# A fused stack of graph layers: another order of blocks on every engine, another table of PSUM banks, another order of loads

## What is computed

```
h  = relu(LN(x));   H = (adj != 0)
x1 = x + hypergraph_conv(LN(relu(hypergraph_conv(h; W1))); W2) + h     # "L0": D^-1 H B^-1 H^T (x W^T)
x2 = x1 + elu(softmax_masked(leaky(a1.Wh + a2.Wh)) Wh),  h = relu(LN(x1))          # "L1", mask adj > 0.5
x3 = x2 + relu(h W0 + T h W1 + T T h W2 + b), T = adj*exp(leaky(si+sj)) normalised  # "L2", h = relu(LN(x2))
x4 = x3 + w v,  w = softmax over nodes of sum_m(q k^T / 8 * adj), h = relu(LN(x3))   # "L3"
```

## Time and profile before

| | |
|---|---|
| median of 3 runs | 1487.95 us (1487.61 to 1488.96) |
| the profiled execution, span | 1487.0 us |
| mean granted TensorE clock | 0.989 |
| busy: PE, DVE, ACT, POOL | 96%, 81%, 66%, 64% |

### The profile page before, as it was taken

The page is one execution under the profiler, slowest core; times in us unless marked ns, Lnnn a source line. Parts: engine busy times, 40 slices in busy tenths (PEclk is TensorE's granted clock), DMA queues, the critical chain, the costliest instruction groups (busy, mean ns, idle before and its releaser), DMA issues.

```text
span 1487.0 us, 33717 instructions
## 1 busy us (share of the span) xinstructions
PE 1423.5 (96%) x8920; PEld 1263.7 (85%) x8920; DVE 1206.8 (81%) x4621; ACT 978.8 (66%) x2122; POOL 949.7 (64%) x974
## 2 busy tenths in 40 slices
PE   6799999999999999999999999999999999999975
PEld 5679988889888988988888988888988888988864
DVE  5778888888888888888888888888888888888773
ACT  4456667766667776667776666776666776666754
POOL 4555775666776666676666676675677666677524
PEclk9899999999999999999999999999999999999997
DMA  4001111101111110111110111110111110111001
GB/s 128 22 15 37 37 42 44 49 32 46 35 48 36 49 47 30 35 49 35 49 49 28 42 42 35 49 49 28 45 39 35 49 49 28 49 35 41 23 29 50
DMA packets 75372, 62.01 MB, mean 42 GB/s; under 512 B 3014, under 2 KB 70986, under 8 KB 75339
## 3 DMA queue, kind: packets, MB, share of 16 engines
q1 hardware_dynamic: 75338, 61.63, 12.7%
HBM read 36.45 MB, written 16.78 MB: 36 GB/s over the span
## 4 chain that ended last, share of the span: by engine, by line
PE 75%; ACT 11%; issue 5%; DVE 5%; DMA 1%; POOL 0%; DVEq 0%; ACTq 0%; POOLq 0%; SPq 0%
PE ps L343 35%; PE ps L347 18%; PE ps L328 16%; PE ps L491 4%; ACT wh L851 3%; ACT pT L940 3%; ACT h L918 2%; ACT h2T_hi L881 1%; ACT p L929 1%; PE ps L400 1%; ACT yT_hi L953 1%; DMA x_in<-in_x 1%; DVE stats L1329 1%; DVE h L1347 1%; DVE binc_T L1368 0%
## 5 line engine op out<-in xcount | busy, mean ns | idle before, releaser
L1130 POOL TENSOR_TENSOR x3n<-p,x 128x512 f32<-128x512 f32 x64 | 80.8, 1285 | 252.8 <-ACT p L929 252.8
L851 ACT ACTIVATE p<-ps,rs 128x512 f32<-128x512 f32 (+1 forms) x256 | 138.2, 582 | 106.4 <-PE ps L347 73.7
L1090 POOL TENSOR_TENSOR hT_lo<-hT,hT_hi 128x512 fp32r<-128x512 f32 x126 | 162.8, 1294 | 68.5 <-ACT hT_hi L871 65.4
L1085 POOL TENSOR_TENSOR rs<-var_e,neg_half 128x4 f32<-128x4 f32 x160 | 164.9, 1031 | 23.7
L343 PE MATMUL ps<-wl_hi,h2T_hi 128*128 128x258 f32 (+1 forms) x512 | 148.5, 371 | 7.8 <-ACT h2T_hi L881 7.2
L328 PE MATMUL ps<-p,alT 128*128 128x256 f32 (+1 forms) x512 | 136.9, 390 | 3.3 <-DVE h3T_lo L1239 2.3
L343 PE MATMUL ps<-wl_lo,h2T_hi 128*128 128x258 f32 (+1 forms) x512 | 132.9, 341 | 0.0
L347 PE MATMUL ps<-wl_hi,h2T_lo 128*128 128x258 f32 (+1 forms) x512 | 132.4, 340 | 0.0
L949 ACT ACTIVATE h3T_hi<-ps 128x512 fp32r<-128x512 f32 x64 | 38.0, 594 | 139.0 <-PE ps L491 138.9
L491 PE MATMUL ps<-ident,h 128*128 128x128 f32 x768 | 118.3, 278 | 9.9 <-DVE h L1347 9.4
L491 PEld LDWEIGHTS ps<-ident,h 128*128 128x128 f32 x768 | 92.3, 142 | 32.9 <-issue 10.4
(11 more groups left out here) (178 smaller groups left out, 4476.0 us busy)
## 6 DMA issues: line engine op xcount, KB each, us to landing
x_in<-in_x SPq DMA_DIRECT2D x32, 512.0 KB, 3.9
out_x<-x SPq DMA_DIRECT2D x32, 512.0 KB, 2.9
adj_f<-in_adjT SPq DMA_DIRECT2D x32, 256.0 KB, 2.9
adj_m<-in_adjT SPq DMA_DIRECT2D x32, 256.0 KB, 2.8
adj_l<-adj_m SPq DMA_DIRECT2D x32, 256.0 KB, 2.3
vqk<-in_l_wk SPq DMA_DIRECT2D x3, 256.0 KB, 5.2
x<-in_w2T SPq DMA_DIRECT2D x1, 512.0 KB, 5.1
x<-in_w1T SPq DMA_DIRECT2D x1, 512.0 KB, 5.9
```

The costliest lines, as they stand in the source:

```text
L851: return act.activation(dst, src, ACT.Copy, scale=scale)
L1085: pool.tensor_tensor(rs[:, layer, :], var_e[:, layer, :], neg_half[:], ALU.pow).then_inc(done, G)
L1090: pool.tensor_tensor(hTs[1][:, hc, :], hT[:, hc, :], hTs[0][:, hc, :], ALU.subtract).then_inc(S["hT_lo"], 1)
L1130: pool.tensor_tensor(x3n[:, s], p0[:, s], x2[:, s], ALU.add).then_inc(S["x3_ready"], 2)
```

## The change

No arithmetic is added or taken away on any engine, apart from how it is cut (relu of p0 in two halves on ACT; each layer norm in two halves of two groups; one more memset for each half).

- PE: the blocks of a round stand in another order (below). Round 0 has its own list, `opening`, in the old order with `first_rows` behind `front_w1(0)`.
- DVE: `elu`, layer norm 2, `mid_low`, layer norm 3, the pooling sums, `mid_columns`, `late_low(0)` and `tail_norm` are done for the coming round at the end of the body (`ahead`); `front_penalty` becomes `next_penalty` and is done one round earlier; count, inverse, binc and moments come first in the body.
- ACT: `copy_h2T(0)` moves ahead of `copy_u(2)`, the copies of vqk 2 and 3 behind the softmax, `copy_p2(3)` behind the exponentials of the edges, `keep_wh(3)` ahead of `copy_yT`, half of relu of p0 ahead of `keep_wh(1)`, the other half behind vqk 3.
- POOL: `add_res0` and `add_x3` of the round before come first; the power pair of the next group stands behind that of the hidden layer and ahead of `mask_edges`; `add_bias` ahead of `add_x4`, both `add_xb` last.
- BANK: every product has other banks, and the waits of PE's blocks follow from the table: for example `mid_p10(2)` waits for `zb_ready`, `late_vqk(0)` for `deg_ready`, `late_vqk(2)` for `wh_kept` 3, `next_y(0)` for `wh_kept` 1, `mid_p2(3)` for `p10_copied` 1 (as before), `front_w1(3)` for the copy of u 0, `front_w1(0)` for both low halves of y.
- SP: the loads wait for the penalty alone in the steady rounds; the order becomes `adj_f`, adj_m to adj_l, `x_in`, store, `adj_m`.

```diff
     PAIRS = G // 2
-    FIRST_STEADY = 4
+    FIRST_STEADY = 6
+    LAST_SHIFT = 4
     ATT = wqkT.shape[1] // 2
     assert C == P and G * C == 512 and GROUPS > FIRST_STEADY + 1
...
         """.split()
         S = {n: sem(n) for n in names}
 
-        BANK = {"u": (0, 4, 3, 2), "y": (0, 7), "s": (4, 5), "d": (0,), "c2": (6, 5), "h1": (7, 1), "wh": (2, 3, 4,
-    5), "b1": (6,), "att": (1, 5), "h2": (4, 3), "p2": (4, 5, 6, 7), "p10": (7, 6, 7, 6), "b2": (5,),
-    "z": (1, 2, 3, 4), "ap": (0, 1, 2, 3), "az": (0, 3), "h3": (0, 5), "vqk": (4, 1, 6, 7), "ak": (6,),
-    "row": (1,), "turn": (7,)}
+        BANK = {"u": (3, 6, 0, 3), "y": (0, 3), "s": (5, 6), "d": (7,), "c2": (0, 7), "h1": (1, 5),
+    "wh": (0, 1, 2, 3), "b1": (5,), "att": (1, 2), "h2": (5, 6), "p2": (2, 3, 4, 5),
+    "p10": (5, 7, 6, 0), "b2": (6,), "z": (0, 1, 2, 3), "ap": (1, 2, 3, 4), "az": (6, 4),
+    "h3": (7, 4), "vqk": (5, 7, 2, 6), "ak": (7,), "row": (6,), "turn": (5,)}
 
         def bank(name, k=0):
...
+        wait(sp, S["al_ready"], r.mid(G))
+    if not r.steady and r.i in (GROUPS - 2, GROUPS - 1, GROUPS,):
+        wait(sp, S["ak_ready"], r.late(G))
+    sp.dma_start(adj_l[:], adj_m[:]).then_inc(S["adj_l_loaded"], 16)
+
+def load_mask(r):
+    if r.steady or r.i > 0:
+        sp.wait_ge(S["adj_l_loaded"], r.loads(r.i - 1))
+    sp.dma_start(adj_m[:], group(adjT, r.i)).then_inc(S["adj_m_loaded"], 16)
+
 def body(r):
-    if r.has_next:
-        if r.steady or r.i >= 0:
-
-            wait(sp, S["pen_ready"], r.front(G))
-            wait(sp, S["binc_ready"], r.front(G))
-            sp.dma_start(adj_f[:], group(adjT, r.i + 1)).then_inc(S["adj_f_loaded"], 16)
-            wait(sp, S["h0_ready"], r.front(G))
-            wait(sp, S["xb_ready"], r.front(G))
-            sp.dma_start(x_in[:], group(x, r.i + 1)).then_inc(S["x_loaded"], 16)
-    if r.has_tail:
-        wait(sp, S["x4_ready"], r.tail(G))
-        sp.dma_start(group(out, r.i - 3), x4[:]).then_inc(S["stored"], 16)
-    if r.has_mid:
-
-        wait(sp, S["al_ready"], r.mid(G))
-        wait(sp, S["ak_ready"], r.late(G))
-        sp.dma_start(adj_l[:], adj_m[:]).then_inc(S["adj_l_loaded"], 16)
-        sp.wait_ge(S["adj_l_loaded"], r.loads(r.i - 1))
-    if r.has_front:
-        sp.dma_start(adj_m[:], group(adjT, r.i)).then_inc(S["adj_m_loaded"], 16)
-
-rounds(sp, body)
+    past = r.later(-1)
+    if r.has_next:
+        load_adj(r)
+    if past.has_mid:
+        hand_adj(past)
+    if r.has_next:
+        load_x(r)
+    if past.has_tail:
+        store(past)
+    if past.has_front:
+        load_mask(past)
+
+def opening(r):
+    load_adj(r)
+    load_x(r)
+
+rounds(sp, body, opening)
 sp.wait_ge(S["stored"], 16 * GROUPS)
 
...
@@ -734,79 +619,77 @@
         front_w1(r, 0)
         front_w1(r, 1)
         front_w1(r, 2)
+    if r.has_mid:
+        mid_h2(r, 0)
+    if r.has_front:
         front_w1(r, 3)
     if r.has_mid:
-        mid_h2(r, 0)
         mid_h2(r, 1)
+        mid_p2(r, 0)
         mid_p10(r, 0)
+        mid_p2(r, 1)
+    if r.has_front:
+        front_w2(r, 0)
+    if r.has_mid:
+        mid_p2(r, 2)
+    if r.has_late:
+        late_h3(r, 0)
     if r.has_tail:
         tail_row(r)
     if r.has_mid:
-        mid_p2(r, 0)
-        mid_p2(r, 1)
-        mid_p2(r, 2)
         mid_p2(r, 3)
     if r.has_front:
-        front_w2(r, 2)
-    if not r.steady and r.i == 0:
-        second_rows(r)
-        first_weights(r)
-    if r.has_front:
-        front_w2(r, 0)
+        front_w2(r, 1)
     if r.has_mid:
         mid_b2(r)
     if r.has_front:
-        front_w2(r, 3)
-        front_w2(r, 1)
         front_w2_low(r, 0)
         front_w2_low(r, 1)
+        front_w2(r, 2)
+        front_w2(r, 3)
         front_w2_low(r, 2)
+        front_w2_low(r, 3)
         front_sums(r, 0)
         front_sums(r, 1)
         front_sums(r, 2)
-        front_w2_low(r, 3)
         front_sums(r, 3)
-    if r.has_mid:
-        mid_p10(r, 1)
-    if r.has_late:
-        late_h3(r, 0)
-    if r.has_mid:
-        mid_p10(r, 2)
     if r.has_late:
         late_h3(r, 1)
     if r.has_mid:
-        mid_ap(r, 0)
-        mid_ap(r, 1)
+        mid_p10(r, 1)
     if r.has_tail:
         tail_turn(r)
     if r.has_mid:
+        mid_p10(r, 2)
+    if r.has_front:
+        front_c2(r, 0)
+        front_c2(r, 1)
+        front_c2(r, 2)
+    if r.has_next:
+        next_s(r, 0)
+        next_s(r, 1)
+    if r.has_mid:
+        mid_ap(r, 0)
+    if r.has_front:
+        front_c2(r, 3)
+    if r.has_mid:
+        mid_ap(r, 1)
         mid_ap(r, 2)
         mid_ap(r, 3)
-    if r.has_front:
-        front_c2(r, 0)
-        front_c2(r, 1)
+        mid_p10(r, 3)
     if r.has_late:
         late_vqk(r, 0)
     if r.has_front:
-        front_c2(r, 2)
-        front_c2(r, 3)
-    if r.has_mid:
-        mid_p10(r, 3)
+        front_h1(r, 0)
     if r.has_late:
         late_vqk(r, 1)
-    if r.has_next:
-        next_s(r, 0)
     if r.has_mid:
         mid_az(r, 0)
+    if r.has_front:
+        front_h1(r, 1)
+    if r.has_mid:
         mid_az(r, 1)
-    if r.has_next:
-        next_s(r, 1)
-    if r.has_front:
-        front_h1(r, 0)
-    if r.has_late:
-        late_vqk(r, 2)
-    if r.has_front:
-        front_h1(r, 1)
+    if r.has_front:
         front_wh(r, 0)
         front_wh(r, 1)
         front_wh(r, 2)
...
         add_x4(r, 0)
-    if r.has_mid:
-        add_bias(r, 0)
-    if r.has_tail:
         add_x4(r, 1)
-    if r.has_front:
-        rsqrt(1, mv[:, 1, :, 1], S["ag1"], r.front(G), S["var1"], S["rs1_ready"])
+    if r.has_next:
+        shift_x(r)
+    if r.has_front:
+        front_scale1(r)
     if r.has_mid:
         add_bias(r, 1)
     if r.has_next:
+        add_xb(r, 0)
         add_xb(r, 1)
-    if r.has_mid:
-        add_x3(r, 0)
-        add_x3(r, 1)
+
+def opening(r):
+    front_lo(r, 0)
+    front_lo(r, 1)
+    add_res0(r, 0)
+    add_squares(r, 0)
+    add_res0(r, 1)
+    add_squares(r, 1)
+    join_squares(r)
+    front_scale0(r)
+    next_scale(r)
+    shift_x(r)
+    add_xb(r, 0)
+    front_scale1(r)
+    wide_lows()
+    add_xb(r, 1)
...
-        first_dots()
-    if r.has_mid:
-        elu_low(r, 0)
-    if r.has_front and (r.steady or r.i > 0):
-        y_low(r.front(G), 1)
-    if r.has_mid:
-        elu_low(r, 1)
-    if r.has_tail:
-        tail_weights(r)
-    if r.has_mid:
-        elu_high(r, 0)
-        elu_high(r, 1)
-        mid_ln2(r)
-        mid_low(r, 0)
-    if r.has_tail:
-        tail_sum(r)
-    if r.has_front:
-        front_penalty(r)
-    if r.has_tail:
-        tail_max(r)
-    if r.has_mid:
-        mid_low(r, 1)
+    ahead = r.later(1)
     if r.has_next:
         next_count(r)
-    if r.has_mid:
-        mid_columns(r)
-    if r.has_next:
-        next_moments(r)
-    if r.has_late:
-        late_ln3(r)
-    if r.has_mid:
-        mid_edges(r)
-    if not r.steady and r.i == 0:
-        second_dots()
-    if r.has_front:
-        front_variance(r)
-    if r.has_tail:
-        tail_norm(r)
-    if r.has_next:
         next_inverse(r)
         next_binc(r)
+        next_moments(r)
+    if r.has_front:
+        front_variance(r)
+    if r.has_mid:
+        mid_edges(r)
     if r.has_late:
-        late_low(r, 0)
+        late_low(r, 1)
+    if r.has_tail:
+        tail_out(r)
     if r.has_front:
         front_z(r, 0)
         front_z(r, 1)
-    if r.has_tail:
-        tail_out(r)
-    if r.has_late:
-        late_low(r, 1)
+        front_z(r, 2)
+        front_z(r, 3)
+        front_residual(r, 0)
+        front_ln1(r, 0)
+        front_residual(r, 1)
+    if r.has_next:
+        next_degrees(r)
     if r.has_mid:
         z1_scale(r)
         mid_z1(r, 0)
+    if r.has_front:
+        front_ln1(r, 1)
+    if r.has_mid:
         mid_z1(r, 1)
     if r.has_front:
-        front_ln1(r)
+        front_low(r, 0)
     if r.has_mid:
         mid_z1(r, 2)
     if r.has_front:
-        front_low(r, 0)
+        front_low(r, 1)
     if r.has_mid:
         mid_z1(r, 3)
-    if r.has_next:
-        degree_bounds(r)
-        degree_inverse(r)
-        degree_masked(r)
-    if r.has_front:
-        front_low(r, 1)
-    if r.has_mid:
         mid_vb(r, 0)
+        mid_vb(r, 1)
     if r.has_front:
         front_columns(r)
     if r.has_next:
@@ -1659,18 +1590,94 @@
         front_logits(r, 0)
         front_logits(r, 1)
         front_leaky(r, 0)
+        front_leaky(r, 1)
         front_max(r, 0)
-        front_leaky(r, 1)
         front_max(r, 1)
-    if r.has_mid:
-        mid_vb(r, 1)
-    if r.has_front:
-        front_inverse(r, 0)
-        front_scale(r, 0)
-        front_inverse(r, 1)
-        front_scale(r, 1)
-    if r.has_next:
-        y_low(r.next(2), 0)
+    if r.has_next:
+        y_low(r, 0)
+    if r.has_mid:
+        mid_vb(r, 2)
+    if r.has_front:
+        front_weights(r, 0)
+        front_weights(r, 1)
+    if r.has_mid:
+        mid_vb(r, 3)
+    if r.has_next:
+        y_low(r, 1)
+    if r.has_front:
+        elu_low(r, 0)
+        elu_low(r, 1)
```

(70 more changed lines are left out.)

617 lines of the change are left out of this document (315 added, 302 removed).

## The result

The changed kernel takes 1492.03 us (median of 9 runs, 1490.10 to 1493.41), the kernel before 1488.17 us beside it (9 runs): ratio 1.0024, 95% interval 1.0015 to 1.0034. It is slower by a little, where 1444.5 us were forecast. The profiled execution has a span of 1490.8 us against 1487.0.

What follows compares the result with a forecast made beforehand. TensorE (PE), busy 96% of the span, was taken as the bound, with its waits removable. 28 rounds at -1.0 us (-28) and the ends (-15.5) take the span from 1487.0 to 1443.5; forecast 1444.5 us, range 1422 to 1474.

Steps and rivals of the forecast that it cites:

- The port: POOL additions beside DVE's two leaky steps, sharing access to SBUF: priced at +0.2 us a round, bounds 0 and 2.2.
- Rival 2: Each leaky step stands still about half a POOL operation, delaying att: 0.9 us a round, 1464 us; chance 0.10.
- rival 4: Nothing moves: stalls come back behind another wait, since DVE's chain sets the round; 1488 us, chance 0.04.
- PE's order: Between h2's pair 0 transposes and their first product stand w1's last block and pair 1, covering a 0.56 us wait.
- The softmax: Ahead of att: pT_scaled found ready 0.4 us before PE asks for it, so att's 0.40 us stall goes.
- The tight covers: Mid-round, z and zb each ready only 0.1 us before PE wants them: 0.1 us a round, bounds 0 and 0.8.
- Rival 1: Both mid-round covers, for z and zb, fail: another 0.8 us lost per round, 1467 us; chance 0.15.
- The load queue: adj_f and x_in issued earlier, once the penalty is done; DVE's wait for adj_f goes: gain 0.1 us a round.
- rival 5: Slower: DVE's stretch ahead of z waits for late-landing x_in; at 3 us late 1528 us; chance 0.07.
- The opening: Penalty ahead of y_low removes DVE's 5.1 us adj_f wait and half of PE's 10.0 for z: -5 us.
- All other new waits on a bank: Other new bank waits name readers mostly done at least 0.3 us earlier: priced at 0, upper end 0.2.
- The drain: End of the run: layer norm 3 starts before the columns, relu and x3 in halves: -8 us, bounds 0 and -11.

Runs made afterwards that it cites:

- a2: Changed kernel with POOL's add_x3 0 waiting until both leaky steps have ended and add_res0 1 put behind it: 1454.67 us, ratio 0.9764.
- b1: Kernel before, with two added two-input POOL additions of 128x512 from SBUF beside the two leaky steps: 1536.09 us, ratio 1.0310.
- c2: Changed kernel with POOL held off the leaky steps and h2's pair 0 put back behind w1's last block: ratio 0.9972.
- a4: Changed kernel with only add_x3 held until both leaky steps have ended; add_res0 1 still runs beside the first: ratio 0.9783.
- c4: Changed kernel with POOL held, DVE's edges ahead of the moments of x, and those split around the variance: 1449.80 us, ratio 0.9733.
- e1: Changed kernel with POOL held and the load queue in the old order, with x_in's two waits in every round: ratio 0.9774.
- b4: Kernel before, with two added one-input POOL operations of 128x512 beside the leaky steps: 1490.1 us in one run, beside 1488.5.
- d3: Changed kernel with POOL held, edges split, the opening reordered, and ACT copying both halves of s ahead of h1T's first pair: 1446.66 us, ratio 0.9710.
- c3: Changed kernel with POOL held; in the opening, DVE's degrees one low half earlier and ACT's keep_wh 3 ahead of the softmax: ratio 0.9752.
- a3: Changed kernel, opening reordered: degrees ahead of layer norm 1 pair 1, keep_wh 3 ahead of the softmax, first rows ahead of w1: ratio 0.9986.
- d2: Changed kernel with POOL held, edges split; opening with s ahead of c2, degrees behind layer norm 1's first half, keep_wh 3 earlier: 1449.02 us, ratio 0.9736.

## Why the prediction was wrong, step by step

The time by pieces, in us of change against the kernel before. POOL held (a2) is the changed kernel without the port's effect.

| piece | forecast | after | POOL held |
|---|---|---|---|
| to w1 of round 1 | -5 | +6.0 | +5.4 |
| rounds 1 and 2 | -2.5 | +1.5 | -2.0 |
| 28 rounds | -28 | -0.5 | -32.0 |
| drain | -8 | -3.1 | -5.3 |
| span | -43.5 | +3.8 | -33.9 |

*The port: the step that failed.* The prediction had the mechanism, the place, the two additions and the cover of 0.4 us, and named bounds of 0 and 2.2 us. It took 0.2, "both steps lengthened as the penalty was when it met POOL, by part of 0.4 each, less the room". The measured price is 1.12 us a round: 1.59 of standing still less 0.47 of cover. The penalty's row was read as a fixed surcharge of 0.4 and not as a remainder. These are the two rows of the kernel before behind it:

```profile
25.96 1.28 POOL L1136 TENSOR_TENSOR res<-xb,h 128x512 f32<-128x512 f32 x1
...
26.69 0.83 DVE L1378 TENSOR_SCALAR pen<-adj_f 128x512 f32<-128x512 f32 x1
```

The penalty began 0.55 us before the end of the addition (27.24) and ended 0.28 behind that end, just as the leaky steps do (0.28 behind in b1: 741.36 and 741.64). It lost 0.4 because only 0.55 of the addition was left. The leaky steps met more: the additions follow one another without a gap, so the second step met a new one as the first ended, and they lost 0.5 and 1.1. Rival 2 at 0.9 a round was close to the 1.12 of this term, and had a chance of 0.10; its time of 1464 is not the measured one, because the opening above all, and the drain, fell short too. The upper end of 2.2, from the earlier trace rows less the cover, was the better guide. The rule of the Trainium skill (SBUF — State Buffer, Who interferes with whom) that the prediction cites is borne out here for additions on two inputs (the leaky step took 1.28 us), and for memsets, which only write SBUF and which the rule leaves free (0.415). The 0.60 and 0.41 beside the one-input operation differ from it, and there the measurement decides. The penalty reads one tensor, so a rule on two inputs does not cover its 0.83 and 0.99 us.

*Near a rival by chance.* The time lies next to the 1488 of rival 4, "nothing moves". Its mechanism, that DVE's chain sets the round, is not what happened: with POOL held the round is 43.17.

*PE's order: the mechanism right, the size too low.* -0.56 was forecast for h2; in the new order the place is worth 0.98 (c2), in which DVE's longer penalty may have a small part. That price holds beside the block of 258 columns which stands there now; the kernel before had blocks of 512, so part of it is not a gain of the change but a cost that the change would have met. Everything in a round but the port gave 44.31 - 43.17 = 1.14, where the forecast has 1.2 + 0.1 - 0.1 = 1.2: the sum was right, its division was not shown.

*The softmax.* pT_scaled 0.4 us ahead of att: right to within 0.1 (0.48 in a4). With POOL in the way the 0.40 did not go, it grew to 1.06.

*The tight covers.* 0.1 a round was taken with bounds of 0 and 0.8. Measured 0.22 (c4), all of it at zb; z held. Rival 1, with 0.8 more, did not happen.

*The load queue.* DVE's wait for adj_f of the earlier trace rows fell from 59.0 to 3.4 us. The time did not follow, and with the old queue it stays the same (e1): 0, not 0.1. The penalty's place in DVE's order did it. No x_in came late ahead of the variance: rival 5 did not happen.

*The opening: wrong in sign.* -5 was forecast from one row, z's 10.0 us. c2 did start 2.0 us earlier (41.72 against 43.75), with 7.0 us less of waiting: the length of that wait was no measure of a delay. The kernel before with the one-input operations (b4) shows the same without any edit ahead of z: 4.5 us of waiting instead of 10.0, and w1 of round 1 at 60.67 instead of 61.45. Behind it the changed opening has a wait of 3.3 for the degrees ahead of h1's pair 1, and of 3.1 for wh 3 ahead of y, both from the new bank table, and the lower clock over wh. "All other new waits on a bank name a reader that my walk finds done" was walked for a steady round only. In the opening every step ahead of the reader stands in another order. Of the 6.0, 2.1 lies ahead of the first w1 (18.50 against 16.38), although the 1.05 us of first_rows no longer stand there. PE waits 1.6 us there for yT_lo, behind the penalty that DVE now does first (0.42), and w1's weights landed in 7.7 instead of 5.9 us; this differs from run to run (6.2 in b4, 6.5 in d3, 7.1 in c3).

*The drain: too large.* h's waits fell from 8.8 to 4.8 us, about as walked. But waits for wex, wrow, vqk and wcol grew beside them, and the sum of all of PE's waits in the drain fell from 17.6 to 14.5 us, by the same 3.1 as the drain. I priced the waits that would go and did not ask, at that end, which is late next.

*The miss in one sum.* The span came out 47.3 us above the forecast. 37.7 of it is the changed kernel less POOL held: the port, 0.2 x 28 = 5.6 of which was in the forecast. 9.6 is left between POOL held and the forecast: 10.4 in the opening, 2.7 in the drain, 0.5 in rounds 1 and 2, less 4.0 in the 28 rounds, where the forecast without its port term is 33.6 of gain against 32.0 measured.

## What to carry to other kernels

Before a VectorE step is moved, write down what GpSimd does in the same microsecond, and price a two-input addition there at its whole remainder. One long row can hold this: compare its end with the end of what ran beside it, not its length with its median. If an engine has to be busy beside the step, hold the other one: one wait on POOL gave 35 us here (a4, by the spans), and 38 with two additions exchanged (a2).

A walk of steady rounds says nothing of the opening, where a new wait on a bank has its reader in another place. There, moving one engine's step can only move the wait (a3, d2), so read the next wait before keeping the move. And the length of a wait is not the time that its removal gives: follow the start of the block behind it.
